# Two idle products on TensorE in front of the last two sums of each layer's edge stage

## The chip, the cores and the metric

The kernel runs on one core of one Trainium2 chip. The metric is the device time of one execution in microseconds (us); the median over several executions counts.

## The reference, cut to what matters

A graph network with four layers over 1250 nodes of 512 features and 40000 edges that are sorted by their destination:

```
for l in range(4):
    m   = relu(x[src] + edge_weight1 @ We[l] + be[l])       # one row of 512 for each edge
    agg = segment_sum(m, dst)                               # added up by destination node
    h   = ((1 + eps[l]) * x + agg) @ W1[l] + b1[l]
    h   = relu(batch_norm over all nodes(h) * gamma[l] + beta[l])
    x   = relu(h @ W2[l] + b2[l])
out = layernorm(x_in + x)
```

The batch norm needs the sums over all nodes, so the second half of a layer can't begin before the last edge is added up, and the next layer's gathers need the new x in memory.

## The kernel before, in words

The nodes are cut into 10 blocks of 128, the edges into tiles of 128. A layer's edge stage is a loop of 10 steps (`edge_step(l, i)`, one on each engine); a step has 32 tiles, the last one (i = 9) has 25. A tile's 128 source rows come into SBUF in one of two ways: GpSimd issues an indirect DMA for it (L793), or, for 95 tiles of a layer, TensorE makes the rows by one-hot products (`gather_tiles`, L1872). No tile of the last step is of the second kind.

The tiles of a step stand in eight quads, 0 to 7. VectorE turns a quad's gathered rows into messages (`messages`, L1446) and raises `v_ready[q]`. TensorE then adds them up (`sum_quad`, L1821): for each tile one product of a 128x32 one-hot matrix with the 128x512 messages, in fp32, into one of four windows of 32 partitions of `pair_ps[0]` (quads 0 to 3) or `pair_ps[1]` (quads 4 to 7). Each such product shows as two matmul records. A product of this form takes 32 of the array's 128 columns, so products for different windows stand side by side. In the last step quads 4 to 7 hold 3, 3, 2 and 1 tiles, made so that the last messages to arrive are the smallest piece of work.

The engines run their instructions in program order. On TensorE the end of the last step is: sums of quad 4, four products that add the first pair, sums of quad 5, 6 and 7, then `idle_products(..., GAP)`: two 128x128 by 128x512 products (L1957) whose result nobody reads. Meanwhile ScalarE copies `pair_ps[1]` to SBUF in two halves (L1037, L1038), and `close_last` (L1921) places the copy into the block's sum; `product_last` (L1936) multiplies by W1; VectorE and ScalarE make the batch norm's statistics and scales; and `dense` begins with four more idle products (`WARM`, also L1957) and goes on with the products by W2 (L1993, L2004), after which the new rows are written to the table in memory and the next layer's gathers begin. The sync queue waits for `quad_summed[6]` before it loads the bias b2 (L738).

The idle products read `src_onehot` and `table_parts` as they stand, in fp32r, and write a PSUM bank that is free at that time. They wait for no semaphore.

Of the kernel before, what the change touches and what calls it, by code (L numbers as in the profile page):

```python
# [27 lines left out]
def gnn_layers(nc, x_pad, src_t, src_late, dst_t, w_t, We, be, W1, W2, b2, vectors, eps, out):  # L28
# [10 lines left out]
    L, D, _ = W1.shape  # L39
# [15 lines left out]
    TAIL = N - (BLOCKS - 1) * P + MARGIN  # L55
    WARM = 4
    GAP = 2
    GUARD = 2 * P
    PLACED = HALF + 2 * MARGIN

# [86 lines left out]
    def is_near(i, tile):  # L147
        return i in SORTED and tile % LONG < nears(LONG_A_STEP * i + tile // LONG)
# [6 lines left out]
    TILES_A_LAYER = len(NEAR_TILES)  # L155
# [13 lines left out]
    def near_through(i, q):  # L169
        return sum((j, p) <= (i, q) for j, p, _, _ in NEAR_TILES)  # L170
# [40 lines left out]
    def tiles_of(quads, h):  # L211
        tiles = [t for q in quads[4 * h:4 * h + 4] for t in q]
        windows = [[t for t in tiles if t[2] == win] for win in range(WINDOWS)]
        return tiles, [w[0] for w in windows], [w[-1] for w in windows]

    ctx = ExitStack()
    with ctx:
        def sb(name, shape, dt=fp32):
            return ctx.enter_context(nc.sbuf_tensor(name, shape, dt))
# [7 lines left out]
        table_parts = sb("table_parts", [P, PARTS, len(NEAR_BLOCKS), D], fp32r)  # L227
        src_bc = sb("src_bc", [P, len(SPREAD_AT), P], u8)
        src_onehot = sb("src_onehot", [P, 2 * ONEHOTS, P], fp32r)
        hT = sb("hT", [P, C, GUARD - MARGIN + BLOCKS * P])  # L230
        W1_sb = sb("W1_sb", [P, C, D])
# [11 lines left out]
        def early(c, k, n=T_PAD):  # L243
            return hT[:, c, GUARD + k:GUARD + k + n]

# [35 lines left out]
        def extra_onehot(e):  # L281
            return hT[:, 1 + e % 3, GUARD:GUARD + (LONG - 1) * P].rearrange("p (j n) -> p j n", n=P)

# [9 lines left out]
        extra_src = sb("extra_src", [P, P], u8)  # L293
        extra_w = hT[:, 0, GUARD:GUARD + 2 * P].bitcast(fp32r).rearrange("p (v n) -> p v n", v=2)
        extra_key = sb("extra_key", [P, len(EXTRAS)], i32)
        extra_ints = sb("extra_ints", [P, 2, len(EXTRAS)], i32)
        extra_values = sb("extra_values", [P, 2, len(EXTRAS)])
        extra_edges = hT[:, 0, GUARD + 2 * P:GUARD + 2 * P + 2 * LONG * len(EXTRAS)].rearrange("p (e j v) -> p e j v", j=LONG, v=2)
        minus_place = hT[:, 0, GUARD + 3 * P:GUARD + 3 * P + LONG * len(EXTRAS)].rearrange("p (e j) -> p e j", j=LONG)
        minus_from = sb("minus_from", [P, 1])  # L300
# [54 lines left out]
        def pb(name, shape):  # L355
            return ctx.enter_context(nc.psum_tensor(name, shape, fp32))
# [5 lines left out]
        y_ps = [pb(f"y_ps{b}", [P, D]) for b in range(3)]  # L362
# [1349 lines left out]
        def _(pe):  # L1712
            pe.wait_ge(sort_dve, NEAR_READY)
            for c in range(KINDS):
                nc.tensor.matmul(before_ps[c], up_to[:, :], near[:, c, :, :], start=True, stop=False, skip_group_check=True)
                for k in range(1, LONG):
                    last = nc.tensor.matmul(before_ps[c][:, :, k:LONG], all_of[:, :], near[:, c, :, 0:LONG - k],
                                            start=False, stop=(k == LONG - 1), skip_group_check=True)
# [31 lines left out]
            for e in range(len(EXTRAS)):  # L1750
                pe.wait_ge(extra_onehot_ready, e + 1)
                for j in range(LONG - 1):
                    last = nc.tensor.matmul(extra_ps[:, e, :], extra_onehot(e)[:, j, :], extra_edges[:, e, j, :],
                                            start=(j == 0), stop=(j == LONG - 2))
# [14 lines left out]
            for v in range(2):  # L1769
                last = nc.tensor.matmul(extra_turned_ps[0:len(EXTRAS), v, :], extra_values[:, v, :], ident[:, :],  # L1770
                                        start=True, stop=True, is_transpose=True)
# [40 lines left out]
            def sum_quad(q, l, i):  # L1812

                h, quad = q // 4, STEPS[i][q]
                _, firsts, lasts = tiles_of(STEPS[i], h)
                pe.wait_ge(v_ready[q], BLOCKS * l + i + 1)
                if any(is_near(i, tile) for _, tile, _ in quad):
                    pe.wait_ge(tile_ready, TILES_A_LAYER * l + near_through(i, q))
                for t in quad:
                    slot, tile, win = t  # L1820
                    last = nc.tensor.matmul(pair_ps[h][WIN * win:WIN * (win + 1), :],  # L1821
                                            onehot[:, h, tile - h * PAIR, :], rows[:, slot, :],
                                            start=t in firsts, stop=t in lasts)
                last.then_inc(quad_summed[q], 1)

            def edge_step(l, i):
                n = BLOCKS * l + i
                final = i == BLOCKS - 1
                for q in range(QUADS):
                    if q % 4 == 0:  # L1830

                        pe.wait_ge(pair_copied[q // 4], n + 1)
                        pe.wait_ge(onehot_ready, 2 * n + q // 4 + 1)
                    sum_quad(q, l, i)
                    if final:
                        gather_tiles(l, QUADS * i + q)
                    elif q % 2:
                        gather_tiles(l, QUADS * i + q - 1)
                        gather_tiles(l, QUADS * i + q)
                    if 0 < i:  # L1840
                        if q == (0 if final else 1):
                            open_block(n - 1, l, i - 1, True)
                            add_first_pair(n - 1, l, i - 1)
                        if q == 1:
                            close_block(n - 1, i - 1)
                        if q == (2 if final else 3):
                            product_h(n - 1, l, i - 1)
                    if q == 0 and l == 0 and i == 0:
                        sum_w(0)
                    if q == 1 and l == 0:  # L1850
                        place_w(i)
                    if q == 3 and final:
                        open_block(n, l, i, True)
                    if q == 4 and final:
                        add_first_pair(n, l, i)
                    if q == 6 and not final and l == 0:
                        sum_w(i + 1)

            def gather_tiles(l, place):

                for k in MADE[l].get(place, []):
                    pe.wait_ge(src_onehot_ready, TILES_A_LAYER * l + k + 1)
                    pe.wait_ge(w_rows[k % len(w_rows)], w_rows_count(l, k))
                    if k == 0:
                        pe.wait_ge(lo_ready, PARTS_A_LAYER * (l + 1))
                        pe.wait_ge(We_rows, 64 * (l + 1))
                        if l:
                            pe.wait_ge(y_added, BLOCKS * l)
                    if k > 1:
                        pe.wait_ge(tile_ready, TILES_A_LAYER * l + k - 1)  # L1870
                    for part, b in PLACES:
                        last = nc.tensor.matmul(y_ps[k % 2][:, :], src_onehot[:, 2 * (k % ONEHOTS) + b, :],  # L1872
                                                table_parts[:, part, 2 * pair_of(k) + b, :],
                                                start=(part, b) == PLACES[0], stop=(part, b) == PLACES[-1])
                    last.then_inc(tile_gathered, 1)

            def open_block(n, l, i, pairs):


                pe.wait_ge(u_ready, n + 1)  # L1880
                pe.wait_ge(uT_copied, n + 1)
                chunks = [slice(c * P, (c + 1) * P) for c in range(C)]
                for c, f in enumerate(chunks):
                    to = sums_of(c, l, i) if pairs else uT_ps[:, c, :]
                    last = nc.tensor.matmul(to, u[:, f], ident[:, :],  # L1885
                                            start=(c == 0 or pairs and i == BLOCKS - 1 and c == C // 2),
                                            stop=not pairs, is_transpose=True, skip_group_check=True)
                last.then_inc(u_turned if pairs else block_summed, 1)
                if not pairs:
                    return  # L1890
                pe.wait_ge(place_ready, n + 1)
                if not i:
                    return
                pe.wait_ge(carry_copied, (BLOCKS - 1) * l + i + 1)
                for c, f in enumerate(chunks):
                    nc.tensor.matmul(sums_of(c, l, i)[:, 0:PLACED - HALF], carry[:, f], place1(i - 1, HALF, PLACED),  # L1896
                                     start=False, stop=False, skip_group_check=True)
# [53 lines left out]
                                                start=(k == 0), stop=(k == C - 1))  # L1951
                last.then_inc(h_summed, 1)

            def idle_products(to, times):

                for _ in range(times):
                    nc.tensor.matmul(to, src_onehot[:, 0, :], table_parts[:, 0, 0, :], start=True, stop=True)  # L1957

            pe.wait_ge(flag_ready, 1)
            slow = pe.value_load(flag[0:1, 0:1], min_val=0, max_val=1)  # L1960
            def edges(l):
                gather_tiles(l, -1)
                for i in range(BLOCKS):
                    edge_step(l, i)
                idle_products(y_ps[1 - TILES_A_LAYER % 2][:, :], GAP)
                close_last(BLOCKS * l + i, l, i)
                product_last(BLOCKS * l + i, l, i)
# [96 lines left out]
```

## Time and profile before

| | us |
|---|---|
| median of 3 runs | 1327.08 |
| lowest and highest run | 1325.04, 1330.03 |
| the profiled execution's own time | 1327.84 |
| its span, first to last instruction | 1326.0 |
| TensorE busy in the span | 1182.2 (89%) |
| VectorE busy in the span | 1035.7 (78%) |
| mean granted clock of TensorE | 0.939 |

Times in the rows below count from the start of the span. In a timeline a line is a run of instructions of one kind: start, length, engine, line, operation, tiles, shape, count and, in brackets, how long the engine sat idle before it and what ended that. The granted clock is 1.00 at TensorE's full 2.4 GHz and 0.50 at 1.2 GHz.

### The profile page before, as it was taken

To read this page: it belongs to the slowest core of one execution; us is meant where nothing else is said; L and a number is where in the kernel's file an instruction comes from. 1 tells how busy PE (TensorE), PEld (TensorE's weight loads), DVE (VectorE), ACT (ScalarE), POOL (GpSimd) and SP (SyncE) were. 2 spreads that over 40 slices of the span, in tenths; PEclk is the share of its full clock that TensorE was granted. 3 is DMA by queue.
4 is the path that set the end of the run, shared out by engine and by line. 5 is a ranking of instruction groups with operands and counts; after the bars stand their busy time and mean duration, and the time that the engine had idled before them with its cause. 6 is when DMAs were issued, how large, how long until landed. Compare 5 with 4: busy or idle time off the path is not lost.

```text
span 1326.0 us, 24625 instructions
## 1 busy us (share of the span) xinstructions
PE 1182.2 (89%) x7214; PEld 730.1 (55%) x7214; DVE 1035.7 (78%) x2107; ACT 506.3 (38%) x1107; POOL 821.5 (62%) x871
## 2 busy tenths in 40 slices
PE   2628999999997999999797999999799899999797
PEld 2624666665643665566353566656454465666463
DVE  7968889898668878787757878787766987778668
ACT  2713434343272343334173343333254333343233
POOL 0057777777327777777607777777705777777720
PEclk7558999999799999999799999999898999999889
DMA  3177777777557777777737777777846777777753
GB/s 110 62 223 215 216 214 215 216 215 214 162 165 218 215 216 215 216 215 216 216 104 232 214 216 214 215 216 215 241 122 199 215 215 215 215 215 215 224 163 124
DMA packets 94297, 263.31 MB, mean 199 GB/s; under 512 B 19739, under 2 KB 22924, under 8 KB 94160
## 3 DMA queue, kind: packets, MB, share of 16 engines
q0 software_dynamic: 68800, 225.50, 58.6%
q1 hardware_dynamic: 25360, 36.19, 8.4%
q8 instruction: 62, 1.02, 0.3%
q14 instruction: 75, 0.61, 0.1%
HBM read 248.46 MB, written 12.96 MB: 197 GB/s over the span
## 4 chain that ended last, share of the span: by engine, by line
POOL 42%; PE 32%; issue 14%; DVE 7%; DMA 3%; ACT 1%; SPq 0%; DVEq 0%
POOL rows L793 42%; PE y_ps L1993 9%; PE y_ps L1872 7%; PE pair_ps L1821 6%; PE h_ps L1950 3%; DVE rows L1356 2%; DVE rows L1446 2%; PE y_ps L2004 1%; DMA rows<-node_table,src_fast 1%; PE uT_ps L1903 1%; PE uT_ps L1910 1%; DMA src_onehot<-near_ws 1%; PE uT_ps L1896 1%; DMA node_table<-rows 1%; PE y_ps L1957 1%
## 5 line engine op out<-in xcount | busy, mean ns | idle before, releaser
L793 POOL DMA_INDIRECT rows<-node_table,src_fast x860 | 818.9, 952 | 449.6 <-issue 262.3
L1446 DVE SCALAR_TENSOR_TENSOR rows<-We_ps,negw_fast,rows 128x512 f32<-128x512 f32 x860 | 593.2, 742 | 180.3 <-DMA rows<-node_table,src_fast 179.4
L1872 PE MATMUL y_ps<-table_parts,src_onehot 128*128 128x512 f32 x1520 | 405.9, 414 | 29.1 <-DMA src_onehot<-near_ws 17.8
L969 ACT ACTIVATE rows<-y_ps 128x512 f32<-128x512 f32 x380 | 224.7, 603 | 536.7 <-PE y_ps L1872 526.3
L1872 PEld LDWEIGHTS y_ps<-table_parts,src_onehot 128*128 128x128 f32 x1520 | 271.6, 191 | 220.0 <-issue 102.5
L1821 PE MATMUL pair_ps<-rows,onehot 128*32 128x512 f32 x2504 | 332.2, 624 | 66.1 <-DVE rows L1446 65.5
L1821 PEld LDWEIGHTS pair_ps<-rows,onehot 128*32 128x32 f32 x2504 | 60.5, 110 | 208.3 <-DVE rows L1446 105.0
L1950 PEld LDWEIGHTS h_ps<-uT,W_sb 128*128 128x128 f32 x1152 | 136.4, 195 | 7.8 <-issue 5.0
L1292 DVE TENSOR_TENSOR src_onehot<-y_ps,src_bc 126x256 fp32r<-126x256 f32 x352 | 137.5, 411 | 0.0
L1950 PE MATMUL h_ps<-uT,W_sb 128*128 128x128 f32 x1152 | 137.3, 278 | 0.0
L1993 PE MATMUL y_ps<-rows,hT 128*128 128x512 f32 x288 | 124.5, 593 | 0.0
L1993 PEld LDWEIGHTS y_ps<-rows,hT 128*128 128x128 f32 x288 | 54.4, 190 | 67.9 <-issue 58.8
L1069 ACT ACTIVATE hT<-hT,bn_bias,bn_scale 128x128 f32<-128x128 f32 x160 | 65.5, 479 | 6.5 <-DVE bn_bias L1492 6.5
L982 ACT ACTIVATE hT<-h_ps,vec 128x128 f32<-128x128 f32 x144 | 41.2, 370 | 58.8 <-PE h_ps L1950 58.8
L956 ACT COPY pair_sb<-pair_ps 128x512 f32<-128x512 f32 x76 | 44.3, 583 | 46.1 <-PE pair_ps L1821 46.1
L1635 DVE TENSOR_TENSOR rows<-y_ps,b_bc 128x512 f32<-128x512 f32 x36 | 24.8, 688 | 40.2 <-PE y_ps L1993 40.2
L1280 DVE TENSOR_TENSOR onehot<-y_ps,local_all 128x512 f32<-128x512 f32 x80 | 53.5, 668 | 0.3
L1903 PE MATMUL uT_ps<-place,pair_sb 128*128 128x96 f32 x304 | 45.1, 293 | 0.0
L1903 PEld LDWEIGHTS uT_ps<-place,pair_sb 128*128 128x128 f32 x304 | 39.7, 203 | 3.4 <-issue 3.4
L1910 PEld LDWEIGHTS uT_ps<-place,pair_sb 128*128 128x128 f32 x288 | 36.7, 200 | 5.8 <-issue 5.8
L1910 PE MATMUL uT_ps<-place,pair_sb 128*128 128x64 f32 x288 | 39.1, 281 | 0.0
L943 ACT ACTIVATE u<-x_now,eps 128x512 f32<-128x512 f32 x40 | 29.2, 730 | 24.2 <-PE uT_ps L1885 24.2
(231 smaller groups left out, 742.6 us busy)
## 6 DMA issues: line engine op xcount, KB each, us to landing
late_rows<-node_table SPq DMA_DIRECT2D x1536, 2.0 KB
rows<-node_table,src_fast POOLq DMA_INDIRECT x860, 3.8
node_table<-rows SPq DMA_DIRECT2D x29, 256.0 KB, 3.7
src_onehot<-near_ws SPq DMA_DIRECT2D x380, 2.0 KB
x_now<-x_pad SPq DMA_DIRECT2D x10, 512.0 KB, 8.2
W_sb<-W SPq DMA_DIRECT2D x4, 1024.0 KB, 5.4
rows<-W SPq DMA_DIRECT2D x16, 256.0 KB, 4.0
out<-rows SPq DMA_DIRECT2D x8, 256.0 KB
```

Of the source, the lines that this page charges most:

```text
L793: nc.gpsimd.indirect_dma_start(rows[:, slot, :], None, table[:, :], bass.IndirectOffsetOnAxis(src_fast[:, t:t + 1], 0)).then_inc(landed[q] ...
L969: nc.scalar.activation(rows[:, slot, :], y_ps[k % 2][:, :], ACT.Relu).then_inc(tile_ready, 1)
L1069: nc.scalar.activation(hT[:, c, at:at + P], hT[:, c, at:at + P], ACT.Relu, bias=bn_bias[:, c:c + 1], scale=bn_scale[:, c:c + 1]).then_inc( ...
L1280: return nc.vector.tensor_tensor(to, cols_ps[:, 0:WIN].unsqueeze(1).to_broadcast([P, tiles, WIN]), local_all[:, at:at + tiles].unsqueeze(2 ...
L1292: nc.vector.tensor_tensor(src_onehot[0:USED, at:at + 2, :], nodes[0:USED, :].unsqueeze(2).to_broadcast([USED, 2, P]), src_bc[0:USED, sprea ...
L1446: last = nc.vector.scalar_tensor_tensor(rows[:, slot, :], We_ps[:, :], negw_fast[:, t:t + 1], row, ALU.mult, ALU.max)
L1821: last = nc.tensor.matmul(pair_ps[h][WIN * win:WIN * (win + 1), :], onehot[:, h, tile - h * PAIR, :], rows[:, slot, :], start=t in firsts, ...
L1872: last = nc.tensor.matmul(y_ps[k % 2][:, :], src_onehot[:, 2 * (k % ONEHOTS) + b, :], table_parts[:, part, 2 * pair_of(k) + b, :], start=( ...
L1903: nc.tensor.matmul(sums_of(c, l, i)[:, 0:PLACED], pair_sb[:, 0, f], place0(i), start=False, stop=False, skip_group_check=True)
L1910: last = nc.tensor.matmul(uT_ps[:, c, HALF:P], pair_sb[:, 1, c * P:(c + 1) * P], place1(i, 0, HALF), start=False, stop=True, skip_group_ch ...
L1950: last = nc.tensor.matmul(h_ps[:, c, :], W1_sb[:, k, c * P:(c + 1) * P], uT[:, k, :], start=(k == 0), stop=(k == C - 1))
L1993: last = nc.tensor.matmul(y_ps[m % 3][:, :], hT[:, c, at:at + P], W2_sb[:, c, :], start=(c == 0), stop=(c == C - 1))
```

## The change

In each layer's last step, before the sums of quad 6 and again before those of quad 7, TensorE issues two idle products into the bank that the two products of `GAP` use too. They stand ahead of `sum_quad`, so ahead of its wait for the messages. `idle_products` is moved up in the file so that `edge_step` can call it; nothing else differs.

```diff
+    BETWEEN = 2
...
+            def idle_products(to, times):
+
+                for _ in range(times):
+                    nc.tensor.matmul(to, src_onehot[:, 0, :], table_parts[:, 0, 0, :], start=True, stop=True)
+
             def edge_step(l, i):
                 n = BLOCKS * l + i
                 final = i == BLOCKS - 1
...
                         pe.wait_ge(pair_copied[q // 4], n + 1)
                         pe.wait_ge(onehot_ready, 2 * n + q // 4 + 1)
+                    if final and q > 5:
+                        idle_products(y_ps[1 - TILES_A_LAYER % 2][:, :], BETWEEN)
                     sum_quad(q, l, i)
```

That makes four products more in a layer and sixteen in the kernel.

## Rows read from the trace of the kernel before

**Rows 1.** The page, the chain that ended last, by engine and by line
```profile
POOL 42%; PE 32%; issue 14%; DVE 7%; DMA 3%; ACT 1%; SPq 0%; DVEq 0%
POOL rows L793 42%; PE y_ps L1993 9%; PE y_ps L1872 7%; PE pair_ps L1821 6%; PE h_ps L1950 3%; DVE rows L1356 2%; DVE rows L1446 2%; PE y_ps L2004 1%; DMA rows<-node_table,src_fast 1%; PE uT_ps L1903 1%; PE uT_ps L1910 1%; DMA src_onehot<-near_ws 1%; PE uT_ps L1896 1%; DMA node_table<-rows 1%; PE y_ps L1957 1%
```

**Rows 2.** Timeline of TensorE, end of layer 0's edge stage
```profile
338.00 1.94 PE L1821 MATMUL pair_ps<-rows,onehot 128*32 128x512 f32 x8
339.87 1.97 PE L1910 MATMUL uT_ps<-place,pair_sb 128*128 128x64 f32 x8
...
352.11 1.06 PE L1821 MATMUL pair_ps<-rows,onehot 128*32 128x512 f32 x6
353.10 0.69 PE L1903 MATMUL uT_ps<-place,pair_sb 128*128 128x96 f32 x4
...
354.16 1.91 PE L1821 MATMUL pair_ps<-rows,onehot 128*32 128x512 f32 x12
356.00 0.72 PE L1957 MATMUL y_ps<-table_parts,src_onehot 128*128 128x512 f32 x2
356.62 0.66 PE L1921 MATMUL uT_ps<-place,pair_sb 128*128 128x64 f32 x4
...
361.34 1.18 PE L1957 MATMUL y_ps<-table_parts,src_onehot 128*128 128x512 f32 x4
362.36 4.09 PE L1993 MATMUL y_ps<-rows,hT 128*128 128x512 f32 x9
```

**Rows 3.** Timeline of TensorE, the same place in layer 3
```profile
1276.20 1.91 PE L1821 MATMUL pair_ps<-rows,onehot 128*32 128x512 f32 x12
1278.04 0.73 PE L1957 MATMUL y_ps<-table_parts,src_onehot 128*128 128x512 f32 x2
```

**Rows 4.** Timeline of TensorE, the same place in layer 1
```profile
658.16 1.06 PE L1821 MATMUL pair_ps<-rows,onehot 128*32 128x512 f32 x6
661.35 2.57 PE L1821 MATMUL pair_ps<-rows,onehot 128*32 128x512 f32 x6 [2.13 <-DVE rows L1446]
663.85 1.22 PE L1957 MATMUL y_ps<-table_parts,src_onehot 128*128 128x512 f32 x2
664.87 0.63 PE L1921 MATMUL uT_ps<-place,pair_sb 128*128 128x64 f32 x4
```

**Rows 5.** Timeline of TensorE, the same place in layer 2
```profile
956.65 1.06 PE L1821 MATMUL pair_ps<-rows,onehot 128*32 128x512 f32 x8 [1.34 <-DVE rows L1446]
...
968.74 2.57 PE L1821 MATMUL pair_ps<-rows,onehot 128*32 128x512 f32 x6 [1.34 <-DVE rows L1446]
971.24 1.17 PE L1957 MATMUL y_ps<-table_parts,src_onehot 128*128 128x512 f32 x2
972.25 0.55 PE L1921 MATMUL uT_ps<-place,pair_sb 128*128 128x64 f32 x4
```

**Rows 6.** Timeline of VectorE, the last messages of layer 0
```profile
346.57 6.00 DVE L1446 SCALAR_TENSOR_TENSOR rows<-We_ps,negw_fast,rows 128x512 f32<-128x512 f32 x9
```

**Rows 7.** Timeline of VectorE, the last messages of layer 1
```profile
659.88 2.07 DVE L1446 SCALAR_TENSOR_TENSOR rows<-We_ps,negw_fast,rows 128x512 f32<-128x512 f32 x3 [2.14 <-DMA rows<-node_table,src_fast]
```

**Rows 8.** Timeline of VectorE, the last messages of layer 3
```profile
1275.15 0.75 DVE L1446 SCALAR_TENSOR_TENSOR rows<-We_ps,negw_fast,rows 128x512 f32<-128x512 f32 x1 [0.45 <-DMA rows<-node_table,src_fast]
```

**Rows 9.** Windows: length, busy PE, PEld, DVE, ACT, POOL, granted clock, DMA share, GB/s
```profile
331.00:347.00 16.00, 15.27 (x70) 10.09 (x71) 10.20 (x17) 1.83 (x3) 12.21 (x13) 0.50 0.83 263
348.00:356.00 8.00, 8.00 (x62) 4.62 (x62) 6.83 (x19) 1.63 (x5) 0.00 (x0) 1.00 0.11 43
...
659.00:661.40 2.40, 0.27 (x5) 0.06 (x4) 1.52 (x3) 0.00 (x0) 0.00 (x0) 1.00 0.02 5
661.70:664.90 3.20, 3.20 (x9) 1.04 (x6) 2.51 (x13) 0.65 (x2) 0.00 (x0) 0.50 0.14 46
665.10:670.00 4.90, 4.88 (x42) 4.71 (x42) 2.60 (x11) 0.85 (x4) 0.00 (x0) 1.00 0.18 66
...
969.00:972.00 3.00, 3.00 (x8) 0.84 (x5) 2.60 (x13) 0.59 (x2) 0.00 (x0) 0.50 0.07 14
```

**Rows 10.** DMA issues: KB each, median us to landing
```profile
b_bc<-b SPq DMA_DIRECT2D x4, 256.0 KB, 3.1
```

**Rows 11.** Timeline of VectorE, the first use of b2 in layer 0
```profile
369.55 0.69 DVE L1635 TENSOR_TENSOR rows<-y_ps,b_bc 128x512 f32<-128x512 f32 x1 [3.73 <-PE y_ps L1993]
```

More of the change, by code:

```diff
@@ L1952, in product_h @@
                 last.then_inc(h_summed, 1)
-            def idle_products(to, times):
-                for _ in range(times):
-                    nc.tensor.matmul(to, src_onehot[:, 0, :], table_parts[:, 0, 0, :], start=True, stop=True)
             pe.wait_ge(flag_ready, 1)
```

## The prediction

> **What bounds the kernel now.** I read the chain that ended last first, then TensorE's timeline at the end of each layer's edge stage, then VectorE's messages there, then the windows with the granted clock. The chain [rows 1] is 42% GpSimd's gathers (L793) and 32% TensorE: most of a layer goes at the pace of the gathers, and its end, from the last sums through the products by W1 and W2 to the table, is a serial chain of TensorE's. The change sits where that chain begins. A microsecond that the last sums of a layer come later is a microsecond for everything behind them, because the next layer's gathers wait for the table; so I count what happens between the sums of quad 5 and the first product of L1921, four times.
>
> The four layers are in two states there. In layer 0 TensorE is late: the nine messages of quads 5 to 7 and before are done at 346.57 + 6.00 = 352.57 [rows 6], and TensorE comes to quad 5 only at 354.16 [rows 2], because its clock stood at 0.50 (1.2 GHz) from 331 to 347 [rows 9]. It then runs all sums of quads 5, 6 and 7, twelve records, without a break. Layer 3 shows the same twelve records in a row at 1276.20, after its last message had ended at 1275.90 [rows 3, 8]. In layers 1 and 2 TensorE is early: it waits 2.13 and 1.34 us for quad 6 [rows 4, 5], whose messages come from a gather that landed late [rows 7]. In that wait it has next to nothing to do (0.27 us busy in 2.40), and right behind it the clock falls from 1.00 to 0.50 [rows 9]: the six records of quads 6 and 7 take 2.5 us at half clock. By 665.1 it is full again.
>
> **The change part by part.** Nothing is removed, no wait is added, no DMA moves. Sixteen products are added, four in a layer, and they need no semaphore: where TensorE is waiting they run inside the wait, where it is late they stand in its way.
>
> *Price of the pieces at full clock.* An idle product: four of them stand between 361.34 and the next product at 362.36, so 1.02 / 4 = 0.255 us, two 0.51 [rows 2]. The two of GAP take 0.62 (356.00 to 356.62), but the product behind them also waits for a copy, so 0.51 is what I take and 0.62 is the upper bound. The sums of one quad, up to four tiles in different windows, followed by a product that takes the whole array: 352.11 to 353.10, 0.99 us [rows 2]. It depends hardly on the tile count, since the windows run side by side: that was a quad of three.
>
> *Layers 0 and 3 (TensorE late).* Before, quads 5, 6 and 7 together take 356.00 - 354.16 = 1.84 us, because one tile of quad 6 runs beside quad 5, and quad 7 beside the other. With full-array products between them each quad stands alone: 0.99 + 0.51 + 0.99 + 0.51 + 0.99 = 3.99 us. That is 3.99 - 1.84 = 2.15 us more, 0.51 of idle products twice and 1.13 of lost overlap. If the overlap were kept, the cost would be 4 x 0.255 = 1.02 (lower bound); with 0.62 for a pair it is 2.37 (upper). I take 2.15, since in every row of sums with a full-array product behind it that product starts after the sums' stream, as at 353.10. Nothing hides it: the copy, L1921 and everything behind wait for quad 7.
>
> The Trainium skill says on its page "TensorEngine Tiling (Array Packing)", section Key Properties, that a change of the tiling mode drains the TensorE, while tiles of one mode run in parallel. This rule speaks against the change, and the rows bear it out with 0.99 against the 1.84 for three quads; without that rule the sum would be 1.02 for such a layer, with it 2.15.
>
> *Layers 1 and 2 (TensorE waits).* The first pair lies wholly in the wait (0.51 in 2.13 and in 1.34 us). The question is the clock. In layer 2 the same idle time of 1.34 us occurs at 955.3 too, and the sums behind it still ran at full clock (1.06 us for 8 records, [rows 5]); so a wait of that length is followed by either level, and with 0.51 us of work in them the waits shrink to about 1.6 and 0.8 us, nearer to TensorE's state ahead of stretches that stayed full. I take it that the clock stays at 1.00. Then from quad 6's messages to the first product of L1921: 0.99 + 0.51 + 0.99 + 0.62 = 3.11 us, against 664.87 - 661.35 = 3.52 and 972.25 - 968.74 = 3.51 before [rows 4, 5]. That is a gain of 0.41 and 0.40: the full clock is worth more than the second pair and the lost overlap, but not by much.
>
> *The rest at nothing.* The sync queue loads b2 when quad 6 is summed. That comes up to 1 us later in layers 0 and 3; it lands some 3.1 us after its issue [rows 10], near 361, and VectorE needs it at 369.55 [rows 11]. If that cover were gone, the cost would be that 1 us.
>
> **Sum.** 2 x 2.15 - 0.41 - 0.40 = +3.5 us. On the profiled execution's own 1327.84 that gives 1331.3 us. That execution lies 0.8 above the median of the runs shown and inside their spread of 5 us, so I leave it there.
>
> **The rivals.**
> *No fall to prevent.* The change does nothing for the clock, because in most executions it would not have fallen in layers 1 and 2: the stay at 955.3 speaks for that, the two falls shown against. Then before, quad 7 starts one message (0.67 us, from 2.07 for three, [rows 7]) behind quad 6 and the pair ends at 0.67 + 0.99 = 1.66; after, 2.49. Each costs 0.83: 4.3 + 1.7 = +6.0, 1333.8 us.
> *The clock falls all the same.* At half clock a quad takes 1.87 (338.00 to 339.87, [rows 2]) and two idle products 1.02 (663.85 to 664.87, [rows 4]): 1.87 + 1.02 + 1.87 + 1.02 = 5.78 against 3.52, +2.3; if the clock comes back at 665 as shown, 3.65 us at half leave 2.13 of it, half of which is 1.07, so 4.72, +1.2. With 4.3: +6.7 to +8.8, 1334.5 to 1336.6 us. For it: 2.13 less 0.51 is still a longer wait than the one that brought the fall in layer 2.
> *Late in all four layers.* If TensorE is late in layers 1 and 2 as well, 4 x 2.15 = +8.6, 1336.4 us. Two of four layers were.
> *Faster.* TensorE waits in all four layers, and the clock falls in each before and in none after. A low stretch as long as layer 1's, some 3.4 us from quad 6 to 665.0 [rows 4, 9], can cost the path at most half, 1.7 us; the warm cost of the change is 0.83, so a layer gains 0.4 to 0.87, all four 1.6 to 3.5: 1324.3 to 1326.2 us. One late layer costs 2.15, so the sign turns only from three or more such layers on; the trace shows two.
>
> **How the numbers follow.** Forecast as summed 0.45, own range 1329 to 1333.5 (the bounds 1.02 and 2.37 in two layers); no fall to prevent 0.20; falls all the same 0.10; late in all 0.10; faster 0.10; something else 0.05. The range 1326 to 1336 holds the forecast, the first rival, half of the second and third and some of the fourth. A measurement of this kernel can tell about 0.5%, 6.6 us, from no change: below 1320.4 or above 1333.7. Slower by more: some 0.04 of the forecast's, 0.09 of the first rival's, 0.07 and 0.07 of the next two, 0.27 in all; faster by more 0.03, for what I have not seen; the same 0.70.
>
> **What would show it.** Right: in a layer without a wait at quad 6 the three quads stand apart with two L1957 records between them, near 4.0 us from quad 5 to the two products of GAP instead of 1.84; in a layer with a wait the two products lie inside it, the granted clock stays 1.00 behind it, and quad 6 to L1921 takes 3.1 us. Wrong: granted clock 0.50 behind the wait in spite of the products; a late layer that grows by about 1 us only (the sums would overlap the idle products); or a total that moves by more than 9 us either way, which no part of this sum can give.

## The result and the profile after

The changed kernel takes 1331.49 us (median of 15 runs, 1325.1 to 1335.7), the kernel before 1325.04 (15 runs, 1318.2 to 1330.03): a ratio of 1.0049 with a 95% interval of 1.0031 to 1.0066, so 6.5 us slower (4.1 to 8.7). The forecast was 3.5 us slower: the sign is right, the size too small by almost half.

In the profiled execution the chain that ended last keeps its shape (compare [rows 1]); the line of the idle products is L1830 now, that of `close_last` L1929.

```profile
POOL 42%; PE 32%; issue 14%; DVE 7%; DMA 3%; ACT 1%; SPq 0%; POOLq 0%; DVEq 0%
POOL rows L794 42%; PE y_ps L1996 9%; PE y_ps L1880 7%; PE pair_ps L1822 6%; PE h_ps L1958 2%; DVE rows L1447 2%; DVE rows L1357 2%; DMA rows<-node_table,src_fast 1%; PE y_ps L2007 1%; PE uT_ps L1911 1%; PE y_ps L1830 1%; DMA src_onehot<-near_ws 1%; PE uT_ps L1918 1%; PE uT_ps L1904 1%; DMA node_table<-rows 1%
```

TensorE's timeline at the end of layer 0's edge stage after the change, the answer to [rows 2]:

```profile
350.67 1.06 PE L1822 MATMUL pair_ps<-rows,onehot 128*32 128x512 f32 x6
351.66 0.74 PE L1830 MATMUL y_ps<-table_parts,src_onehot 128*128 128x512 f32 x2
352.33 1.05 PE L1822 MATMUL pair_ps<-rows,onehot 128*32 128x512 f32 x4
353.31 0.74 PE L1830 MATMUL y_ps<-table_parts,src_onehot 128*128 128x512 f32 x2
353.98 1.04 PE L1822 MATMUL pair_ps<-rows,onehot 128*32 128x512 f32 x2
354.96 0.74 PE L1830 MATMUL y_ps<-table_parts,src_onehot 128*128 128x512 f32 x2
355.54 0.66 PE L1929 MATMUL uT_ps<-place,pair_sb 128*128 128x64 f32 x4
```

The twelve records of sums that stood in one run of 1.91 us are now three groups of 6, 4 and 2, each followed by the next instruction 0.98 to 0.99 us after its start, although they hold three tiles, two and one. From the start of quad 5 to L1929 it takes 355.54 - 350.67 = 4.87 us, where 356.62 - 354.16 = 2.46 stood before [rows 2]: 2.41 us more. Layer 1 (657.15 to 662.01) takes 4.86 as well.

Layer 2, the answer to [rows 5], first on TensorE, then by windows with the granted clock (columns as in [rows 9]):

```profile
963.75 0.72 PE L1830 MATMUL y_ps<-table_parts,src_onehot 128*128 128x512 f32 x2
966.78 1.05 PE L1822 MATMUL pair_ps<-rows,onehot 128*32 128x512 f32 x4 [2.32 <-DVE rows L1447]
967.77 0.89 PE L1830 MATMUL y_ps<-table_parts,src_onehot 128*128 128x512 f32 x2
968.59 1.92 PE L1822 MATMUL pair_ps<-rows,onehot 128*32 128x512 f32 x2
970.43 1.22 PE L1830 MATMUL y_ps<-table_parts,src_onehot 128*128 128x512 f32 x2
971.45 0.62 PE L1929 MATMUL uT_ps<-place,pair_sb 128*128 128x64 f32 x4
```

```profile
963.80:966.70 2.90, 0.67 (x5) 0.24 (x2) 1.38 (x3) 0.00 (x0) 0.00 (x0) 1.00 0.03 10
966.80:968.10 1.30, 1.30 (x5) 0.42 (x6) 1.30 (x6) 0.00 (x0) 0.00 (x0) 1.00 0.00 0
968.30:971.50 3.20, 3.20 (x6) 1.06 (x6) 1.34 (x8) 0.65 (x2) 0.00 (x0) 0.50 0.46 164
```

The pair lies inside the wait, as forecast, and still the clock falls to 0.50, from some 968.2 on. Quad 7, now alone, takes 1.84 us at it. From quad 6 to L1929 that is 971.45 - 966.78 = 4.67 us against 3.51 before. In layer 3 the same happened one quad earlier: TensorE waited 1.98 us for quad 5, and the clock fell about 1 us after that wait had ended, so that quad 6 (from 1276.48) ran at half clock. No pair stands in that wait; the first one comes behind it.

```profile
1274.40:1275.30 0.90, 0.90 (x6) 0.09 (x6) 0.90 (x2) 0.00 (x0) 0.00 (x0) 1.00 0.00 0
1275.50:1278.70 3.20, 3.20 (x7) 0.89 (x8) 3.02 (x14) 0.00 (x0) 0.00 (x0) 0.50 0.00 0
```

### The profile page after: what moved, and what is told of

Read it like the earlier page. It is cut to its first block, busy times and chain, and to the rows that moved or that the text cites. A ratio compares the mean times of both kernels' runs of the same rounds, so it can differ in the third digit from the quotient of the medians.

```text
span 1329.2 us, 24657 instructions
## 1 busy us (share of the span) xinstructions
PE 1186.5 (89%) x7230; PEld 730.1 (55%) x7230; DVE 1035.6 (78%) x2107; ACT 506.0 (38%) x1107; POOL 820.4 (62%) x871
## 3 DMA queue, kind: packets, MB, share of 16 engines
q8 instruction: 62, 1.02, 0.3%
## 4 chain that ended last, share of the span: by engine, by line
POOL 42%; PE 32%; issue 14%; DVE 7%; DMA 3%; ACT 1%; SPq 0%; POOLq 0%; DVEq 0%
POOL rows L794 42%; PE y_ps L1996 9%; PE y_ps L1880 7%; PE pair_ps L1822 6%; PE h_ps L1958 2%; DVE rows L1447 2%; DVE rows L1357 2%; DMA rows<-node_table,src_fast 1%; PE y_ps L2007 1%; PE uT_ps L1911 1%; PE y_ps L1830 1%; DMA src_onehot<-near_ws 1%; PE uT_ps L1918 1%; PE uT_ps L1904 1%; DMA node_table<-rows 1%
```

## The experiments

All edits are to the changed kernel unless said otherwise. Each total is against runs of the kernel before on the same chip. Where a layer is told as late, TensorE does not wait for quad 6. For the layers that wait, the time from the end of quad 7's message on VectorE to the first product of `close_last` is used; the message's end is read from VectorE's timeline of the run. In the kernel before it was 664.87 - 661.95 = 2.92 us in layer 1 [rows 4, 7].

**The pair before quad 6 alone, and before quad 7 alone.**

```diff
-                    if final and q > 5:
+                    if final and q == 6:      # e1; q == 7 in e2
```

> The pair of idle products stands before quad 6 alone. Theory (lost overlap): quads 6 and 7 stand side by side again; in a layer without a wait, from the start of quad 5 to the first L1929 product 0.99 + 0.67 + 0.99 + 0.58 = 3.2 us, against 2.46 before and 4.87 with the change: +0.8 us a layer, and in a layer that waits for quad 6 next to nothing, so 0 to +3 us over the kernel before. Rival (the products' own stream is the price): half of the change's cost, 3.7 us in such a layer, +3.2 us in all.

> The pair stands before quad 7 alone. Lost overlap: quads 5 and 6 in two rounds 1.84, then 0.67 + 0.99 + 0.58 = 4.1 us in a layer without a wait, +1.6 us; in a layer that waits for quad 6 the pair comes after the wait and lies on the path, +1.0 us; +4 to +6 us in all, more than the pair before quad 6. Rival (own stream): the same as the pair before quad 6, +3.2 us.

Measured: e1 1325.46 us, ratio 1.0006 (0.9990 to 1.0023), so +0.8 us (-1.3 to +3.0). e2 1327.69 us, 1.0021 (0.9998 to 1.0044), +2.8 us (-0.3 to +5.8), lower than the 4 to 6 expected of it, though the interval takes most of that in. TensorE in layer 0 and layer 1 of e1:

```profile
354.11 1.06 PE L1822 MATMUL pair_ps<-rows,onehot 128*32 128x512 f32 x6
355.10 0.74 PE L1830 MATMUL y_ps<-table_parts,src_onehot 128*128 128x512 f32 x2
355.76 1.06 PE L1822 MATMUL pair_ps<-rows,onehot 128*32 128x512 f32 x6
356.75 0.74 PE L1830 MATMUL y_ps<-table_parts,src_onehot 128*128 128x512 f32 x2
357.38 0.66 PE L1929 MATMUL uT_ps<-place,pair_sb 128*128 128x64 f32 x4
```

```profile
661.33 1.70 PE L1822 MATMUL pair_ps<-rows,onehot 128*32 128x512 f32 x6 [1.26 <-DVE rows L1447]
...
663.55 0.66 PE L1929 MATMUL uT_ps<-place,pair_sb 128*128 128x64 f32 x4
```

and layers 0 and 3 of e2:

```profile
355.48 1.90 PE L1822 MATMUL pair_ps<-rows,onehot 128*32 128x512 f32 x10
...
359.53 0.66 PE L1929 MATMUL uT_ps<-place,pair_sb 128*128 128x64 f32 x4
...
1281.09 1.05 PE L1822 MATMUL pair_ps<-rows,onehot 128*32 128x512 f32 x4 [0.26 <-DVE rows L1447]
...
1284.30 0.66 PE L1929 MATMUL uT_ps<-place,pair_sb 128*128 128x64 f32 x4
```

In e1 the six records of quads 6 and 7 stand together in 0.99 us, and the late layer takes 3.27 us (expected 3.2; by the products' own stream 3.7). Quads 5, 6 and 7 still take two passes of 0.99 us, 1.98 us against 1.84 before, so most of the 0.81 us more is the pair's own 0.67. In e2 the same pair costs twice as much, 4.05 us (expected 4.1): quad 7, one tile, has to go through the array by itself in a third pass. With the same number of products the price depends on which quads are parted. In e1 both layers that wait, 1 and 2, run on at full clock, and from the end of quad 7's message (659.87 + 2.07 = 661.94) to L1929 it is 1.61 us instead of 2.92. So where the pair before quad 6 met a wait, the clock stayed full; in each late layer it costs 0.8 us; and the total of +0.8 us fits the two about cancelling. In layer 1 of e2, where no pair stands before quad 6, the clock fell in a wait of 2.92 us. In its layer 3, which waits at full clock, quad 6 to L1929 takes 1284.30 - 1281.09 = 3.21 us where e1 takes 663.55 - 661.33 = 2.22: parting quad 7 costs 0.99 us in a layer that waits.

**The order of the change with almost no stream.** The products between the quads are 16 columns long; those of `GAP` and `WARM` stay as they are.

```diff
+            def thin_products(to, times):
+
+                for _ in range(times):
+                    nc.tensor.matmul(to, src_onehot[:, 0, :], table_parts[:, 0, 0, 0:16], start=True, stop=True)
...
-                        idle_products(y_ps[1 - TILES_A_LAYER % 2][:, :], BETWEEN)
+                        thin_products(y_ps[1 - TILES_A_LAYER % 2][:, 0:16], BETWEEN)
```

> The idle products have 16 columns of moving data in place of 512; the order of the work is the change's. Lost overlap: three quads alone at 0.99, two thin pairs at some 0.25 each and 0.58 give 4.0 us in a layer without a wait, +1.6 us, so some two thirds of the change's cost: +3 to +6 us in all. Rival (own stream): 16 of 512 columns cost 0.1 us or less a pair, 2.7 us in such a layer, +1 us in all or less.

Measured: 1329.83 us, ratio 1.0037 (1.0015 to 1.0059), +4.9 us (2.0 to 7.8). Layer 0, where the thin products have line L1835 and `close_last` L1934:

```profile
354.27 1.06 PE L1822 MATMUL pair_ps<-rows,onehot 128*32 128x512 f32 x6
355.26 0.39 PE L1835 MATMUL y_ps<-table_parts,src_onehot 128*128 128x16 f32 x2
355.58 1.05 PE L1822 MATMUL pair_ps<-rows,onehot 128*32 128x512 f32 x4
...
358.44 0.66 PE L1934 MATMUL uT_ps<-place,pair_sb 128*128 128x64 f32 x4
```

A thin pair takes 0.32 us (355.26 to 355.58), yet the layer takes 4.17 us: 1.71 of the change's 2.41 us are there with hardly any stream: 1.11 because the quads take three passes (0.99 + 0.98 + 0.98 = 2.95 us instead of 1.84), and the two thin pairs' 0.64, less 0.04 at the end. In layer 1 of this run the clock fell in the wait for quad 6 too, and the sums from 662.65 on ran at half clock. The rival, 1 us or less in all, lies outside the interval.

**No full-array product between the quads.** One product in the form of the sums, into the window that quads 6 and 7 leave free, before quad 6 only:

```diff
+            def narrow_products(to, times):
+
+                slot, tile, win = STEPS[BLOCKS - 1][5][2]
+                for _ in range(times):
+                    nc.tensor.matmul(to[WIN * win:WIN * (win + 1), :], onehot[:, 1, tile - PAIR, :], rows[:, slot, :],
+                                     start=True, stop=True)
...
-                    if final and q > 5:
-                        idle_products(y_ps[1 - TILES_A_LAYER % 2][:, :], BETWEEN)
+                    if final and q == 6:
+                        narrow_products(y_ps[1 - TILES_A_LAYER % 2], 1)
```

> One idle product in the form of the sums (128x32, fp32), in the one window that quads 6 and 7 leave free, stands before quad 6; no full-array product stands between the quads. Lost overlap: 2.46 us in a layer without a wait, as before, so 0 us; where TensorE waits, it fills 0.87 us of the wait, and if that keeps the clock full, 0.4 to 1.2 us are gained there: 0 to -3 us in all. Rival (own stream): +0.9 us in each layer without a wait, +2 to +3.5 us in all.

Measured: 1323.29 us, ratio 0.9981 (0.9965 to 0.9997), 2.5 us faster than the kernel before (0.4 to 4.6). Layers 0 and 1 (L1836 is the narrow product, L1936 `close_last`):

```profile
354.42 1.48 PE L1822 MATMUL pair_ps<-rows,onehot 128*32 128x512 f32 x10
355.32 0.59 PE L1836 MATMUL y_ps<-rows,onehot 128*32 128x512 f32 x1
355.73 0.60 PE L1822 MATMUL pair_ps<-rows,onehot 128*32 128x512 f32 x2
...
356.93 0.66 PE L1936 MATMUL uT_ps<-place,pair_sb 128*128 128x64 f32 x4
```

```profile
658.16 1.06 PE L1822 MATMUL pair_ps<-rows,onehot 128*32 128x512 f32 x6
659.06 1.02 PE L1836 MATMUL y_ps<-rows,onehot 128*32 128x512 f32 x2
659.94 1.76 PE L1822 MATMUL pair_ps<-rows,onehot 128*32 128x512 f32 x6
...
662.22 0.66 PE L1936 MATMUL uT_ps<-place,pair_sb 128*128 128x64 f32 x4
```

In the late layer the narrow product's records lie among those of the sums (the first at 355.32, with sums at 355.73 still behind it), and the layer takes 2.51 us, 0.05 more than before. In layer 1 the clock stays full, and quad 7's message (it ended at 658.48 + 2.13 = 660.61) is 1.61 us ahead of L1936, as in e1. The price of the change is gone. Whether the narrow product also keeps the clock is not shown: quad 6 follows the end of quad 5's pass here by only 659.94 - 659.15 = 0.79 us, in layer 3 by 0.62, and in e2, e5 and e9 the clock stayed full over gaps of 0.33 to 0.94 us with nothing in them. So the total is measured, but what brings it is not in this profile.

**Both kernels once more, for more layers.**

> The kernel before, profiled once more, for four more layers. If the state of a layer's end differs by execution, other layers are late or wait than in the first profile; from the start of quad 5 to the first product of L1921: 2.46 us in a layer without a wait. From the end of quad 7's message to that product: near 1.6 us in a layer that waits at full clock, 2.9 us where the clock falls in the wait (2 of 2 in the first profile). Theory (the fall is common in a wait): at least half of the waiting layers show the fall. Rival (the fall is rare): none does.

> The changed kernel, profiled once more. Theory (the pair in the wait does not reliably keep the clock, two of two waits fell in the first profile): one or more waiting layers fall again; a layer without a wait takes 4.9 us from quad 5 to L1929, as before. Rival (the two falls were chance): no fall in any waiting layer, and 2.5 us from the end of quad 7's message to L1929 there.

e5 took 1322.47 us, e6 1336.16. In the kernel before (e5) layer 0 is late with 2.46 us again. Layers 1, 2 and 3 wait for quad 6:

```profile
658.99 2.57 PE L1821 MATMUL pair_ps<-rows,onehot 128*32 128x512 f32 x6 [2.17 <-DVE rows L1446]
...
965.00 1.05 PE L1821 MATMUL pair_ps<-rows,onehot 128*32 128x512 f32 x4 [0.58 <-DVE rows L1446]
...
1271.16 1.70 PE L1821 MATMUL pair_ps<-rows,onehot 128*32 128x512 f32 x6 [0.60 <-DVE rows L1446]
```

The 2.57 us of the first is half clock, the 1.05 (quad 6 alone) and 1.70 are full clock. So one of three fell, which is neither theory as I had put it: the fall goes with the longer waits, and which layers have one differs by execution. In the changed kernel (e6) no layer waits for quad 6 at all: all four take 4.86 to 4.87 us from quad 5 to L1929, as here in layer 0, and the question of e6, whether the clock falls in a wait, had no wait to be tried on.

```profile
355.51 1.06 PE L1822 MATMUL pair_ps<-rows,onehot 128*32 128x512 f32 x6
...
360.38 0.66 PE L1929 MATMUL uT_ps<-place,pair_sb 128*128 128x64 f32 x4
```

**Four products before quad 6.** e1 with `BETWEEN = 4`.

> Four idle products in place of two, before quad 6 alone. Own stream: two more at 0.255, so in a layer without a wait 3.28 + 0.51 = 3.8 us from quad 5 to L1929; where TensorE waits longer than 1.2 us for quad 6 nothing is added and the clock stays: +0 to +3 us over the kernel before, 1 us over two before quad 6. Rival (the clock is what counts and four keep it better than two): no slower than with two before quad 6.

Measured: 1323.9 us, ratio 1.0010 (0.9989 to 1.0031), +1.3 us (-1.5 to +4.1). Layer 0:

```profile
349.96 1.06 PE L1822 MATMUL pair_ps<-rows,onehot 128*32 128x512 f32 x6
350.95 1.20 PE L1830 MATMUL y_ps<-table_parts,src_onehot 128*128 128x512 f32 x4
352.08 1.06 PE L1822 MATMUL pair_ps<-rows,onehot 128*32 128x512 f32 x6
...
353.70 0.55 PE L1929 MATMUL uT_ps<-place,pair_sb 128*128 128x64 f32 x3
```

3.74 us, as expected (3.8). Four products between sums take 1.13 us (350.95 to 352.08) and two 0.67, so a product adds 0.23 and the break itself some 0.2. The waiting layers of this run kept the full clock. Against two products the totals can't be told apart, so the rival of this run stays open.

**A version from what was found.** The narrow product, and six full-array idle products in the wait before quad 0 of the last step, where the four column groups stand empty anyway and no quads are parted (e8); then the six alone (e9). The change's pairs are out in both.

```diff
                 for q in range(QUADS):
+                    if final and q == 0:
+                        idle_products(y_ps[1 - TILES_A_LAYER % 2][:, :], 6)
                     if q % 4 == 0:
```

> The narrow product before quad 6, and six idle products (1.5 us at full clock) in the wait before quad 0 of the last step, behind which the clock of the kernel before is low for 7 to 17 us in every layer. If late layers are late because of that low stretch: fewer late layers, the end of quad 7's message to the first product of L1921 near 1.6 us in most layers in place of 2.8 to 4.0, 2 to 6 us faster than the kernel before. Rival (six products do not keep the clock through waits of up to 4.9 us, or TensorE is held by the gathers anyway): same as the narrow product alone, -2.5 us, or slower where the six lie on the path.

> The six idle products before quad 0 of the last step alone, nothing before quads 6 and 7. If both parts act, by the clock in two different waits: between the kernel before and the two together, -2 to -4 us, and a fall of the clock in the waits before quad 6 in one layer or more, 2.9 us from the end of quad 7's message to the first product of L1921 there. Rival (the narrow product adds nothing once the clock is kept early): the same as the two together, -5 us.

Measured: e8 1318.67 us, ratio 0.9962 (0.9948 to 0.9977), 5.0 us faster than the kernel before (3.0 to 6.9). e9 1320.41 us, 0.9985 (0.9971 to 0.9999), 2.0 us faster (0.1 to 3.8). The narrow product alone gave 2.5, on another chip; with these intervals that is in line with two parts that add. Windows of e8 behind the wait before quad 0, in layers 0, 1, 2 and 3 (to be held against 0.50 in layer 0 in [rows 9]):

```profile
331.00:347.00 16.00, 15.26 (x124) 10.59 (x124) 12.90 (x21) 3.45 (x8) 12.18 (x13) 1.00 0.86 278
636.00:646.00 10.00, 10.00 (x48) 6.42 (x44) 8.50 (x13) 1.33 (x3) 7.56 (x9) 0.50 0.79 251
941.50:944.80 3.30, 3.30 (x17) 1.74 (x16) 2.60 (x4) 0.52 (x1) 2.39 (x4) 0.52 0.75 196
945.00:951.00 6.00, 5.09 (x41) 3.19 (x42) 4.41 (x7) 1.11 (x3) 4.48 (x6) 1.00 0.89 299
1247.00:1258.00 11.00, 11.00 (x52) 6.42 (x44) 9.11 (x14) 1.83 (x3) 8.41 (x9) 0.50 0.81 253
```

In layer 0 the clock stays at 1.00, and the layer's end is no longer late; in the nine profiles without the six the same stretch shows 0.50 to 0.79, in e9 1.00 as well. In layers 1, 2 and 3, where TensorE still idled 3.42, 2.63 and 2.98 us behind the six, the clock fell, in layer 2 for some 3.5 us only; layers 1 and 3 are still late. So the rival is right for three of four layers. In e9, layer 1 has a wait of the kind that the narrow product was meant for:

```profile
656.58 2.57 PE L1822 MATMUL pair_ps<-rows,onehot 128*32 128x512 f32 x6 [1.62 <-DVE rows L1447]
...
660.02 0.55 PE L1936 MATMUL uT_ps<-place,pair_sb 128*128 128x64 f32 x4
```

With nothing in it the clock falls in a wait of 1.62 us, and from the end of quad 7's message (655.11 + 2.07 = 657.18) to L1936 it is 2.84 us. No profile with the narrow product has a wait as long.

## Why the prediction was right in sign and short in size

**The time itself.** The forecast time of 1331.3 us lies next to the measured 1331.49, and that is luck: the forecast started from 1327.84, the kernel before has a median of 1325.04, and the change cost 3 us more than forecast. The upper end of the forecast's own range does not follow from the bounds it names: 1.02 and 2.37 in two layers, less 0.81, give +1.2 to +3.9, so 1329.1 to 1331.8 and not 1333.5.

**Late layers: right, a little low.** The mechanism held to the record: parted quads take 0.98 to 0.99 us each whatever they hold, and nothing hides it. The step gave +2.15, the traces +2.41. The term that was mis-sized is the idle pair, 0.67 us between sums instead of 0.51, twice: I had read it off four products that other full-array products surround. The lost overlap is 1.11 of the 2.41 us, where the sum had 1.13; the rest is the two pairs. The thin products (1.71 us) show that most of the price is there with hardly any stream, and the narrow product (0.05) that it goes when no full-array product stands between the quads. The rule of the Trainium skill, "TensorEngine Tiling (Array Packing)", Key Properties, agrees with these numbers: tiles of one form run in parallel, and a change of form ends that.

**Waiting layers: the step that failed.** "I take it that the clock stays at 1.00" gave -0.41 and -0.40. In the profile of the changed kernel the clock fell behind the one wait for quad 6 in spite of the pair, as in the second rival: 4.67 - 3.51 = +1.16, where that rival had said +1.2. That the two agree so well is partly luck, since the rival had the clock low from quad 6 on, and here quad 6 still ran at full clock. With the measured prices in the sum's own places, 2 x 2.41 + 2 x 1.16 = +7.1 us, against 6.5 measured (4.1 to 8.7); the 1.16 is from one layer and stands for both. Where the first pair alone stood (e1), the clock did stay in both waiting layers, for a gain of 1.3 us in each. The second pair has no wait to lie in and takes 0.99 us of that back (e2, layer 3), so even with the clock kept only 0.3 us is left, 3.21 us against 3.52, where the sum had 3.11.

**Two late layers of four: not a constant.** The forecast took the state of each layer from one execution. The kernel before showed two late and two waiting layers, then one and three; the changed kernel two late, one that waited for quad 6 and one that waited for quad 5, then four late. The third rival, late in all four, was seen in e6 (a single run of 1336.16 us; that the rival said 1336.4 is luck again, for the run is 12.4 us above the median of the kernel before on its chip, and four late layers make 4 x 2.41 = 9.6 of that). The pair itself can make a layer late: it ends 1.66 us after quad 5 begins, and a message that comes earlier than that meets no waiting TensorE. In e6 it did not: in all four layers quad 6's messages were done before quad 5's sums were. How often each state comes was not settled; two profiles of each kernel are too few, and how much of the 6.5 us falls to each kind of layer stays open with it.

**No fall to prevent** is not what the profiles show: of the five waits for quad 6 in the two profiles of the kernel before, three brought a fall, those of 2.13, 1.34 and 2.17 us, and two did not, 0.58 and 0.60 us. All profiles together say more for the pair than the changed kernel alone. Counted from the end of quad 5's pass to quad 6, the gaps with nothing in them were 0.33, 0.65, 0.67 and 0.94 us at full clock, and 1.41, 1.70, 2.20, 2.23 and 2.99 us with a fall (in front of another quad 1.34 us stayed full, [rows 5]). With the pair in them 1.83 and 1.99 us (e1) stayed full and 3.03 us (the changed kernel) fell; with four products 1.19 and 2.58 us (e7) stayed full; with the thin pair 2.62 us (e3) fell. So the rows speak for idle products that keep the clock in such a gap, as the change meant; in the one gap of 3.03 us the pair did not. **Faster** never came for the change. It came for e4, e8 and e9; that it came in e4 by the mechanism that rival had named, a prevented fall, is not shown.

## What to carry to other kernels

Idle work that is to keep TensorE's clock belongs where the engine would wait in any case, in the form of its neighbours: products that use different column groups share the array, and full-array products between them part that work into more passes, here three in place of two. A place that is a wait in one execution can be the path in the next, so cost such work for both and look at more than one profile. Read the price of an operation from a row with the same neighbours.

## What the runs showed that was not expected

Two full-array idle products take 0.51 us among their like, 0.67 us between sums of 128x32, and four take 1.13 there; even a 16-column pair takes 0.32. And the clock can fall after the wait, when TensorE is busy again: in layer 2 of the changed kernel it stood at 1.00 through the wait and through the sums of quad 6 that began at 966.78, and was at 0.50 from 968.3 on. So a wait can be paid for by the work behind it.
